# Second mixture layer: tokens of experts 1 to 3 gathered by DMA, second w2 buffer, comparisons spread over the g_l operations, fewer router products

## What is computed

```python
N = 1024; E = 4; H = 1024; capacity = 256
logits = flat_x @ Wg + bg                       # (1024, 4)
top_vals, top_idx = top_k(logits, 2)
probs = softmax(logits where in the top two, else -inf)
for i in range(E):
    score = where(token i chosen, probs[:, i], -inf)
    sel_p, sel_idx = top_k(score, 256)          # the 256 best tokens of this expert
    p = where(isfinite(sel_p), sel_p, 0)
    tok = flat_x[sel_idx]                       # gather
    y = gelu(tok @ W1[i]) @ W2[i] * p
    out = out.at[sel_idx].add(y)                # scatter back
x = layernorm(x + out)
```

## Time and profile before

| | us |
|---|---|
| median of three runs | 714.93 |
| the profiled execution | 713.89 |
| its span, first to last instruction | 712.2 |
| PE busy | 610.8 (86%) |
| DVE busy | 525.2 (74%) |
| ACT busy | 353.5 (50%) |
| POOL busy | 144.1 (20%) |
| the second mixture, from 565.9 to the end | 146.3 |

### The profile page before, as it was taken

How to read it: one execution, slowest core, us unless ns; L and a number is a source line. 1 busy time by engine, 2 the same in 40 slices (tenths; PEclk the granted TensorE clock), 3 DMA queues, 4 the chain that set the end, 5 groups by cost and what they waited for, 6 DMA issues and landing times. The chain is left out here.

```text
span 712.2 us, 13062 instructions
## 1 busy us (share of the span) xinstructions
PE 610.8 (86%) x4908; PEld 428.8 (60%) x4908; DVE 525.2 (74%) x1046; ACT 353.5 (50%) x678; POOL 144.1 (20%) x268
## 2 busy tenths in 40 slices
PE   3899999995599999849889999999998449999985
PEld 2745555554378888748644444444445228988985
DVE  5788888865757776675598999999946787667425
ACT  3227777771344334411217888888884322544530
POOL 4244555550112222123200111111110000000000
...
DMA packets 23272, 42.48 MB, mean 60 GB/s; under 512 B 12992, under 2 KB 14384, under 8 KB 21936
## 3 DMA queue, kind: packets, MB, share of 16 engines
...
q10 hardware_dynamic: 1088, 0.13, 0.1%
...
## 5 line engine op out<-in xcount | busy, mean ns | idle before, releaser
L466 ACT ACTIVATE probs<-ps 128x512 f32<-128x512 f32 x448 | 213.4, 563 | 79.5 <-PE ps L383 79.0
L359 PE MATMUL ps<-k_stack,q_stack 62*128 62x512 f32 x448 | 175.0, 468 | 7.3 <-DVE row_max L559 3.0
L383 PE MATMUL ps<-q_stack,k_stack 64*128 64x512 f32 x448 | 161.0, 437 | 10.0 <-ACT probs L466 6.3
L562 DVE TENSOR_REDUCE row_max<-ps 128x1 f32<-128x1024 f32 x128 | 149.9, 1214 | 16.9 <-PE ps L359 16.9
L383 PEld LDWEIGHTS ps<-q_stack,k_stack 64*128 64x128 f32 x448 | 76.4, 190 | 82.4 <-ACT probs L466 65.3
L398 PE MATMUL ps<-probs,v_ones 128*32 128x256 f32 (+7 forms) x2048 | 116.3, 344 | 1.8 <-POOL probs L517 1.1
L359 PEld LDWEIGHTS ps<-k_stack,q_stack 62*128 62x128 f32 x448 | 80.5, 200 | 37.6 <-DVE row_max L562 16.8
L559 DVE CUSTOM_DVE_ANT_0 y_sums<-ps,wide_mask 128x1024 f32<-128x1024 f32 (+7 forms) x128 | 91.3, 754 | 13.8 <-PE ps L359 12.7
L398 PEld LDWEIGHTS ps<-probs,v_ones 128*32 128x32 f32 x2048 | 51.4, 110 | 44.4 <-issue 14.1
L517 POOL TENSOR_SCALAR_AFFINE_SELECT probs<-probs 128x128 f32<-128x128 f32 x128 | 38.1, 303 | 48.2 <-ACT probs L466 46.7
L866 POOL TENSOR_TENSOR w_chunk_l_m<-y_sums,w_chunk_h_m 128x512 fp32r<-128x512 f32 (+1 forms) x24 | 24.2, 1032 | 104.7 <-ACT w_chunk_h_m L924 97.4
(11 more groups left out here) (201 smaller groups left out, 1182.5 us busy)
## 6 DMA issues: line engine op xcount, KB each, us to landing
y_sums<-in_w_experts SPq DMA_DIRECT2D x8, 1024.0 KB, 4.8
...
q_stack<-part_rows SPq DMA_DIRECT2D x32, 64.0 KB, 4.0
k_stack<-part_rows SPq DMA_DIRECT2D x32, 64.0 KB, 4.0
q_stack<-max_rows SPq DMA_DIRECT2D x128, 2.0 KB
```

The lines of the kernel that those rows point to most:

```text
L359: mm = pe.matmul(scores_bank(s, a, b), stack("q_stack", h, slice(0, TOP))[:, qt * P:(qt + 1) * P], stack("k_stack", h, slice(0, TOP))[:, a ...
L383: pe.matmul(bank(at % 3, 0, b - a), stack("k_stack", h, slice(0, SIDE))[:, kt * P:(kt + 1) * P], stack("q_stack", h, slice(0, SIDE))[:, a: ...
L466: act.activation(probs[:, t % 4, a:b], bank(at % 3, 0, b - a), ACT.Exp).then_inc(exp_done, 1)
L562: dve.tensor_reduce(row_max[:, h % 2, qt:qt + 1], scores_bank(s, 0, end), AX.X, ALU.max).then_inc(scores_free, 1)
```

## The change

- **Gather.** x is written to a DRAM buffer `x_rows` at the start of the block. A third and fourth column of `slot_cols` carry each token's number, so that `slots(e)` also gives every slot's token; `take_slots` writes them as integers, and POOL issues two indirect DMAs (128 rows of 1 KB each) into `x_slots`. `turn_slots(e+1)`, four 128x128 transposes, takes the place of `gather(e+1)` and stands inside the down product of expert e, three quarters of the way through. Expert 0 is still gathered by matmuls (`gather_first`), which now start with the first block of `one_hot` instead of the eighth.
- **Order on PE.** `slots(e+1)` goes up to behind piece 1 (piece 2 for expert 0). `ranks(e+2)` goes to behind the down product of expert e, and `ranks(1)` behind piece 0 of expert 0. In `ranks(0)` 14 matmuls of 512 columns are added whose result nobody reads (`keep_warm`).
- **Order on DVE.** The comparisons of expert e+2 stand one by one behind the g_l operations of expert e, the last five behind the fourth. `assign(e+2)` stands behind the scaling of expert e. The low part of the first w1 and of x change places.
- **Buffers.** w2 has two buffers; the parts of x share the memory of w1's second one. Semaphores of w1 and w2 are apart.
- **Router, both mixtures.** The high and low part of the router's weights lie side by side as one stationary operand, so that 8 matmuls of 512 columns do what 12 did; the two parts are added when the result is turned, by a matmul with a folding matrix. The top-two chain loses one step, and the score no longer needs one of its own (the weights are used as they are). The scores are turned by fp32r matmuls instead of fp32 transposes; ACT copies both halves out.

The core of the diff:

```diff
     def products(self, pe):
-        pe.wait_ge(self.low_ready, 1)
+        pe.wait_ge(self.low_ready, 2)
...
-                mm = product(pe, self.rows[n], (self.high[:, r], self.low[:, r]),
-                             (self.mem["xt_h"][:, k, cols], self.mem["xt_l"][:, k, cols]), k == 0, k == KD - 1)
+                pe.matmul(self.rows[n], self.parts[:, k, :, :].rearrange("p l e -> p (l e)"), self.mem["xt_h"][:, k, cols],
+                          start=k == 0, stop=False, skip_group_check=True)
+                mm = pe.matmul(self.rows[n][0:self.e, :], self.parts[:, k, 0, :], self.mem["xt_l"][:, k, cols],
+                               start=False, stop=k == KD - 1, skip_group_check=True)
...
-        w_h, w_l = sb("w_h", [P, 3, KD * H1], F32R), sb("w_l", [P, 3, KD * H1], F32R)
-        x_h, x_l = sb("x_h", [P, NT, D], F32R), sb("x_l", [P, NT, D], F32R)
+        w_h, w_l = sb("w_h", [P, 4, KD * H1], F32R), sb("w_l", [P, 4, KD * H1], F32R)
+        x_h, x_l = [w[:, 1, :].rearrange("p (t d) -> p t d", t=NT) for w in (w_h, w_l)]
...
+            sp.dma_start(dram["x_rows"].rearrange("(t p) d -> p t d", p=P), x[:, :, :]).then_inc(rows_out, 16)
...
+            pool.wait_ge(rows_out, 16)
+            for e in range(E1):
+                if e:
+                    pool.wait_ge(token_ready, e + 1)
+                    for s in range(ST):
+                        pool.indirect_dma_start(x_slots[:, s, :], None, dram["x_rows"],
+                                                bass.IndirectOffsetOnAxis(ap=slot_token[:, e % 2, s:s + 1], axis=0)).then_inc(slots_in[s], 16)
...
-                if n and e:
-                    act.wait_ge(down_ready, e)
-                act.activation(w_h[:, 2 if n else e % 2, :], raw[:, n, :], ACT.Copy).then_inc(w_high, 1)
+                if n and e >= 2:
+                    act.wait_ge(down_ready, e - 1)
+                act.activation(w_h[:, W_AT(e, n), :], raw[:, n, :], ACT.Copy).then_inc(w_high[n], 1)
...
+            def keep_warm(n):
+
+                for _ in range(n):
+                    pe.matmul(bank(UP), xt[0][:, 0, 0:P], xt[0][:, 0, 0:HALF], start=True, stop=True)
...
+                    if e == 0:
+                        keep_warm((3, 2, 2, 2, 1, 1, 1, 2)[a])
...
+            def gather_first():
+
                 pe.wait_ge(xl_ready, 1)
-                pe.wait_ge(hot_ready, NT * (e + 1))
                 for k in range(KD):
                     for t in range(NT):
+                        if k == 0:
+                            pe.wait_ge(hot_ready, t + 1)
...
+            def turn_slots(e):
+
+                pe.wait_ge(xgl_ready, e)
+                for s in range(ST):
+                    pe.wait_ge(slots_in[s], 16 * e)
+                    for k in range(KD):
+                        mm = pe.transpose(bank(XG, k * CAP + s * P, P), x_slots[:, s, k * P:(k + 1) * P], consts[:, C_ID:C_ID + P])
+                mm.then_inc(gathered, 1)
...
                     turn_hot(e, q)
-                    if q == 1 and e + 1 < E1:
-                        ranks(e + 1)
-                if e + 1 < E1:
-                    slots(e + 1)
-                if e + 1 < E1:
-                    gather(e + 1)
-                pe.wait_ge(w_low, 2 * e + 2)
+                    if e == 0 and q == 0:
+                        ranks(1)
+                    if e < LAST and q == (1 if e else 2):
+                        slots(e + 1)
+                pe.wait_ge(w_low[1], e + 1)
...
+                        if s == 1 and m == MT1 // 2 and e < LAST:
+                            turn_slots(e + 1)
...
                 mm.then_inc(down_ready, 1)
+                if e + 2 < E1:
+                    ranks(e + 2)
...
-                    if q == 1 and e + 1 < E1:
-                        assign(e + 1)
-                if e + 1 < E1:
-                    take_slots(e + 1)
+                    if e == 0 and q == 0:
+                        weights_low(0, 1)
+                    if e + 2 < E1:
+                        compare(e + 2, q, q + 1 if q < NQ - 1 else NT)
+                    if e < LAST and q == (1 if e else 2):
+                        take_slots(e + 1)
+                if e < LAST:
                     weights_low(e + 1, 0)
-                    compare_next(e + 2, 0, C1)
                     split_slots(e + 1)
...
+                    scale(e, 0)
+                    if e + 2 < E1:
+                        assign(e + 2)
                     weights_low(e + 1, 1)
```

215 lines of the change are left out of this document (109 added, 106 removed).

## The result

The kernel with the change takes 693.99 us at the median of four runs (691.27 to 695.01); the kernel before took 715.26 beside it. The ratio is 0.9695, with a 95% interval of 0.9661 to 0.9728: 3.0% faster, 4.4 us slower than the 689.6 predicted. The profiled execution took 694.77 us, against 713.89 before, so the profile holds 19.1 of the 25.3 us that the sum had.

The account below looks back on a forecast made before the run. Bounds: needless work on PE, and waits that also lower its clock. Terms -1.3 - 4.8 + 0.4 - 10.5 - 7.4 - 0.7 - 1.0 = -25.3 from 713.89 give 688.6, as median 689.6; range 683 to 700.

Parts of the forecast that it names:

- A half-clock stretch after 600: Listed sign of a wrong forecast; for experts 1 and 2 it expected PE's clock at 1.00.
- the 2.1 forecast: Expert 0: PE reaches the transposes 2.9 us after the tokens, the gather lands after 5.0, so PE waits 2.1 us.
- 12 x 0.424 = 5.1 us: Second mixture's head: cost at half clock of the 12 added matmuls ahead of the last rank matmul.
- What it buys: the clock is up when `gather_first` starts: Benefit claimed for `keep_warm`: the gather's second half takes 1.9 us, first up product at 593.6 instead of 598.42.
- until 596: Before expert 0: if the clock stays low until then, the first up product comes at 596.5 instead of 593.6.
- Eight fp32r matmuls ... 0.9 us: Second mixture's head: turning the scores by fp32r matmuls of 128 columns at half clock takes 0.9 us instead of 1.88.
- the term of -0.66 for the router: Second mixture: the second copy of the logits no longer waits 0.66 us for PE.
- most of it is on the path: First mixture's router: most of the 1.4 us from four fewer matmuls shortens the time; -1.3 taken (0 to -1.7).
- DVE's top-two follows later: First mixture's router: the doubt for which -1.3 was taken instead of 1.4 us.
- B: Rival, 0.15: clock falls between the experts, costing 5.2 us, plus 2.9 for a cold first gather: 697.
- C: Rival, 0.14: gather lands late, after 8.7 us: 699.5; or 7.3 if DVE holds POOL up: 695.
- rival D: Rival, 0.05: slower than before, gather very late in three down products; decides from a landing of 13.8 us on.

Follow-up runs that it names:

- matmul_gather: one_w2 with the tokens of experts 1 to 3 gathered by 32 matmuls again, at the place of the transposes: 703.84 us, ratio 0.9860.
- grouped: Kernel after, with all comparisons of expert e+2 behind the fourth g_l operation instead of one by one: 700.70 us, ratio 0.9803.
- one_w2: Kernel after, with a single w2 buffer as before instead of two: 695.74 us, ratio 0.9718.
- the repeat: The kernel after, run once more unchanged to show the spread: 695.26 us, ratio 0.9718.
- both: Kernel after without `keep_warm`, and with the second mixture's scores turned by eight transposes and a DVE addition instead of fold matmuls: 690.58 us, ratio 0.9664.
- narrow_warm: Kernel after, with `keep_warm` matmuls of 8 stationary columns instead of 128: 692.69 us, ratio 0.9679.
- late_gather: Kernel after, with four fills of an unused tile on POOL (3.14 us together) ahead of each pair of gathering DMAs: 702.29 us, ratio 0.9827.
- pool_w2: Kernel after, with the low part of each w2 made on POOL instead of DVE: 706.18 us, ratio 0.9890.

## Why the prediction was right or wrong, step by step

Each step by the profile of the kernel after, forecast and measured change in us:

```
                                              forecast  measured
first mixture, with its router                  -1.3      -0.4
norm to the first comparison                    -3.4      -2.6
first comparison to the first up product        -1.4      +1.3
expert 0                                        +0.4      -0.1
expert 1                                       -10.5      -9.2
expert 2                                        -7.4      -7.7
expert 3                                        -0.7      -1.0
way back                                        -1.0      -0.2
stages that the change does not touch            0        +0.7
sum                                            -25.3     -19.2
```

**The experts: right.** The gather as a DMA, the comparisons spread over the g_l operations and the order of slots and ranks take 17.9 us out of experts 0 to 3, against 18.2 forecast. By part: the gather's matmuls 9.3 (matmul_gather), the interleaving 5.1 (grouped, experts 0 and 1), the second w2 buffer 0.7 (one_w2, expert 3); the other 2.8, the order of slots and ranks and the clock, were not taken apart. DVE bounds expert 0, as predicted. Expert 1 it does not: the count had DVE at 17.2 and PE at 16.6, and at full clock PE is busy for all of its 16.87 us and DVE for 16.2. The two were close, so the number held. Expert 2 is PE's. Of expert 1's missing 1.3, the repeat and three further profiles at full clock, with 16.85 to 16.87, show that it is the clock. "A half-clock stretch after 600" was named as a sign of being wrong, and it came, in both experts.

**The gather's landing: right, by luck in part.** 5.0 us after the tokens was forecast and 5.1 measured. It was made up as two issues of 0.53, two of 0.75 for the lists and 2.4 for the landing. Measured are 1.02 until POOL starts, 1.05 and a gap of 0.30, and 2.74 from the second one's start to its landing. The first DMA with its list was priced well (1.28 for 1.35) and the landing nearly (2.4 for 2.74). But the second issue was counted beside a landing that already runs from its start, 1.28 too much, and POOL's start at nothing, 1.02 too little; the two cancel. (POOL's start took 0.43 in experts 1 and 2.) In expert 0 PE waits for 0.29, not the 2.1 forecast, since half clock in that expert brings it there later, 17.1 us after the first up product instead of 15.7; at full clock (both) it waits 1.4.

**From the first comparison to the first up product: wrong, and this is the main miss.** The step that failed is "12 x 0.424 = 5.1 us", about 1.3 us behind DVE, and then "What it buys: the clock is up when `gather_first` starts". The 0.424 for each is right, but seven times the load of 128 stationary columns came on top, 0.19 each by narrow_warm, 1.3 us: with it 2.6 for the 1.3 forecast, and DVE waited 3.0. The other 0.4 is about what the small rank matmuls took over the 1.2 given for them (1.56, from the start times on PE). The router's matmuls, from which I took the price, have 4 stationary columns. The two extra matmuls behind the last rank matmul, and `row` behind them, were put at nothing: they held the gather's start up by another 1.07. And the clock was at half for the first 3.4 us of `gather_first` (590.25 to 593.62), so the benefit was not had. I had kept the case of a low clock "until 596" as a bound with 596.5, and 597.36 came. Without `keep_warm` the stretch from first comparison to first up product takes 14.85 us, against 18.34 with it and 17.03 before. DVE's comparisons of expert 1, by which the forecast had the low part of `xg` late, bound nothing: DVE waited 1.19 for ACT there, and PE for nothing.

**The head: right in kind, 0.8 too much.** The step "Eight fp32r matmuls ... 0.9 us" held (1.02 for the eight of L1268). What failed is the term of -0.66 for the router: the fold matmuls were counted at nothing. They take 1.94 us for sixteen records at full clock and 3.57 at half, and the transposes of before 1.0. DVE's copies of the products end 12.29 us after the norm to 13.22 before, a gain of 0.9 for the 0.66 forecast; from there to the logits it is 1.44 to 0.50, which spends it. The logits stand 13.73 us after the norm, to 13.72 before.

**The first mixture's router: half.** The logits came 1.06 earlier (17.40 to 18.46), near the 1.4 of the four matmuls, but the mixture ends 0.4 earlier. The prediction's "most of it is on the path" failed, and its own doubt about DVE ("DVE's top-two follows later") was the better half of the sentence.

**The way back: a size.** 16.68 at 0.90 of the clock, as before: the half-clock stretch came again, at full length, where I had taken half of it. In the profiles in which it did not come, the way back took 15.2 to 15.4 us, near the 15.1 worked out for full clock. So it either comes or does not, and half of it was a mean of the two.

**Rivals.** B's first half (a cold gather) came true in kind; it cost 1.5 us (5.4 against 3.9 in the repeat), not 2.9. Its second half (the clock falls between experts) came in part: 1.5 us, in expert 0 or in expert 1, in most profiles. C did not come, but its sub-way, DVE holding POOL up, was put down too lightly: I had weighed that `weights_low` goes at 1.1 ns an element, no faster than other operations. late_gather shows that it holds the DMA_INDIRECT up, 2.20 to 0.97 us, and pool_w2 shows the same lock from the other side. The Trainium skill (SBUF — State Buffer, section "SBUF: two separate sides") lists, beside the two-port modes on which my argument stood, a VectorE operation with two SBUF inputs against a GpSimd one that reads SBUF; this trace agrees with the longer list, and with the page's word that the other is blocked until the first is done (4.25 us for an operation of 0.16). It differs in one point: a DMA_INDIRECT that came first did not hold up the DVE operation beside it. C's own landings of 7.3 and 8.7 us were not run; late_gather, with 11.3 in expert 0, cost 8 to 9 us. The 10.9 us that rival D estimated for a DMA of 128 rows did not come: 1.05.
